# Score products as two 64-row tiles of TensorE's array, and the constant rows of the keys written by DMA

## The reference

```python
x = x + 0.5 * ffn(layernorm(x))
x = x + attn(layernorm(x))
x = x + 0.5 * ffn(layernorm(x))

# ffn: 8 experts, each takes the 128 tokens with the highest gate value
affinity = softmax(x @ gate_w)
gating, index = top_k(affinity_T, 128)
h = silu(x_sel @ Wg) * (x_sel @ Wu)
x_out = zeros.at[b_idx, index].add((h @ Wd) * gating)

# attn: 16 heads of 8 features
inner, outer, v = x @ Wi, x @ Wo, x @ Wv
attn = softmax(inner @ outer.T / scale) * aperture * expression
attn = attn / (attn.sum(-1) + 1e-8)
combined = rotate(attn @ v)              # a rotation of pairs, times factors of each head
return combined @ Wout
```

## Time and profile before

| | us |
|---|---|
| median of 3 runs (517.5 to 518.35) | 518.32 |
| span of the profiled execution | 516.1 |
| TensorE busy | 427.1 |
| VectorE busy | 400.4 |
| ScalarE busy | 239.9 |
| GpSimd busy | 68.6 |

### The profile page before, as it was taken

The page is one execution under the profiler, slowest core; times in us unless marked ns, Lnnn a source line. Parts: engine busy times, 40 slices in busy tenths (PEclk is TensorE's granted clock), DMA queues, the critical chain, the costliest instruction groups (busy, mean ns, idle before and its releaser), DMA issues.

```text
span 516.1 us, 7820 instructions
## 1 busy us (share of the span) xinstructions
PE 427.1 (83%) x2252; PEld 250.8 (49%) x2252; DVE 400.4 (78%) x841; ACT 239.9 (46%) x439; POOL 68.6 (13%) x105
## 2 busy tenths in 40 slices
PE   2605999995588899999999999999996506999995
PEld 2501557773454445555555545554553402567773
DVE  6698848899689987778777777777655598768884
ACT  2400443330341267777676777766784201543332
POOL 5510002149000010000000000000002500001100
PEclk9999999998788799999999999999999655999999
DMA  5000012210058810111111111110110000012212
GB/s 166 1 0 1 1 30 62 61 31 0 4 213 276 297 61 25 37 37 43 42 42 42 42 42 42 42 42 1 35 31 0 0 0 2 1 33 59 61 32 81
DMA packets 24749, 26.03 MB, mean 50 GB/s; under 512 B 3634, under 2 KB 16438, under 8 KB 24726
## 3 DMA queue, kind: packets, MB, share of 16 engines
q1 hardware_dynamic: 24726, 25.74, 16.0%
HBM read 16.16 MB, written 9.44 MB: 50 GB/s over the span
## 4 chain that ended last, share of the span: by engine, by line
PE 69%; DVE 25%; issue 3%; ACT 2%; DMA 1%; DVEq 0%; ACTq 0%
PE ps L1133 12%; PE ps L1158 12%; PE ps L1148 10%; DVE neg_max L807 6%; PE ps L999 5%; PE ps L1035 5%; DVE heads_out L707 3%; PE ps L1018 3%; PE ps L1020 3%; PE ps L1019 3%; DVE values L704 3%; PE ps L1050 2%; PE ps L1051 2%; PE ps L960 2%; DVE probs L746 2%
## 5 line engine op out<-in xcount | busy, mean ns | idle before, releaser
L807 DVE TENSOR_REDUCE neg_max<-ps 128x1 f32<-128x512 f32 x256 | 163.4, 684 | 38.9 <-PE ps L1133 38.9
L597 ACT ACTIVATE probs<-ps 128x512 f32<-128x512 f32 x256 | 137.8, 598 | 64.6 <-PE ps L1148 62.9
L1133 PE MATMUL ps<-k_stack,q_stack 128*128 128x512 f32 x256 | 113.7, 452 | 4.8 <-DVE neg_max L807 3.5
L1148 PE MATMUL ps<-q_stack,k_stack 128*128 128x512 f32 x256 | 100.6, 403 | 0.2 <-ACT probs L597 0.2
L1133 PEld LDWEIGHTS ps<-k_stack,q_stack 128*128 128x128 f32 x256 | 49.0, 192 | 68.8 <-DVE neg_max L807 61.7
L1158 PE MATMUL ps<-probs,v_ext 128*32 128x512 f32 x512 | 68.2, 605 | 0.0
L1148 PEld LDWEIGHTS ps<-q_stack,k_stack 128*128 128x128 f32 x256 | 47.7, 190 | 12.7 <-ACT probs L597 5.7
L523 ACT CAST k_stack<-ps 128x512 fp32r<-128x512 f32 x32 | 17.2, 589 | 67.7 <-PE ps L999 67.7
L451 POOL TENSOR_TENSOR w_lo<-w_gu,w_hi 128x512 fp32r<-128x512 f32 x16 | 20.4, 1279 | 149.7 <-ACT w_hi L510 149.7
L769 DVE TENSOR_TENSOR vae_and_gates<-heads_out,ps 128x512 f32<-128x512 f32 x32 | 21.9, 687 | 19.7 <-ACT heads_out L531 17.7
L746 DVE TENSOR_TENSOR probs<-slot_row,slot 128x1024 f16<-128x1024 f16 x32 | 36.5, 1216 | 0.1
(11 more groups left out here) (151 smaller groups left out, 574.8 us busy)
## 6 DMA issues: line engine op xcount, KB each, us to landing
parts_dram<-part_hi SPq DMA_DIRECT2D x8, 512.0 KB, 3.6
parts_dram<-part_lo SPq DMA_DIRECT2D x8, 512.0 KB, 4.9
q_stack<-parts_dram SPq DMA_DIRECT2D x32, 128.0 KB
k_stack<-parts_dram SPq DMA_DIRECT2D x32, 128.0 KB
w_gu<-in_L_ffn_Wg_dram SPq DMA_DIRECT2D x16, 128.0 KB, 2.1
w_gu<-in_L_ffn_Wu_dram SPq DMA_DIRECT2D x16, 128.0 KB, 2.2
wd_sb<-in_L_ffn_Wd_dram SPq DMA_DIRECT2D x16, 128.0 KB, 2.2
x<-in_L_attn_x_dram SPq DMA_DIRECT2D x4, 256.0 KB, 3.8
```

What stands on the lines that cost most here:

```text
L597: nc.scalar.activation(probs[:, u // HG, u % HG, :], ps[:, RING + ring_bank(step, u), :], ACT.Exp, scale=SCORE_SCALE).then_inc(probs_ready, 1)
L807: nc.vector.tensor_reduce(neg_max[:, g, qt, col:col + 1], ps[:, ring_bank(step, u), :], AX.X, ALU.max, negate=True).then_inc(max_taken, 1)
L1133: nc.tensor.matmul(ps[:, ring_bank(step, u), :], q_stack[:, g, pp, chunk(qt)], k_stack[:, g, 2 * pp + jj, :], start=True, stop=True).then_ ...
L1148: nc.tensor.matmul(ps[:, RING + ring_bank(step, u), :], k_stack[:, g, j, chunk(c)], q_stack[:, g, j // 2, :], start=True, stop=True).then_ ...
```

## The change

The score products use 64 rows instead of 128. `q_stack` and `k_stack` become the two halves of one tensor, in which the even head of a pair has rows 0 to 63 and the odd head rows 64 to 127: 32 rows of parts, 31 rows that are zero in the keys, and row 63 (127) with the ones in the keys and the maxima in the queries. The score products take all 64 rows, the maximum products the first 63, so that the row of the maxima needs no clearing. A product's rows fix the part of the array that it uses. The maxima are taken in another order (`max_unit`), so that a score product and the maximum product behind it lie in different halves. The constant rows are written once by four DMAs on SP's queue, from a row of 64 ones and from a zero row in DRAM; GpSimd's three fills of `k_stack` and the clearing DMAs go. `place` gets memory of its own, and the picked tokens lie in both stacks.

```diff
+    PARTS = 4
+    ROWS = PARTS * DH
+    TILE = P // 2
+    MAX_ROW = TILE - 1
...
+        ones_row = sb("ones_row", [1, 64])
-        q_stack = sb("q_stack", [P, G, PAIRS, S], F32R)
-
-        k_stack = sb("k_stack", [P, G, HG, S], F32R)
+        stacks = sb("stacks", [P, 2, G, PAIRS, S], F32R)
+        q_stack, k_stack = stacks[:, 0], stacks[:, 1]
+        place = sb("place", [P, 2, B, S], F32R)
...
+        def max_unit(u):
+
+            return u // HG, (u + 1) % HG
...
             def load_max_rows(n, g):
 
                 sp.wait_ge(max_rows_ready, n + 1)
                 for jj in range(2):
-                    sp.dma_start(q_stack[64 * jj + 32:64 * jj + 33, g].bitcast(F32),
+                    sp.dma_start(q_stack[TILE * jj + MAX_ROW:TILE * jj + TILE, g].bitcast(F32),
                                  max_rows[2 * jj:2 * jj + 2, g % 2, :].bitcast(F32)).then_inc(max_rows_loaded[g], 16)
 
-            sp.wait_ge(scattered[0], B)
-            sp.wait_ge(zero_rows_stored, 16)
-            sp.wait_ge(attention_consts, 3)
-            for g in range(G):
-                clear_max_rows(g)
+            sp.wait_ge(consts_made, 7)
+            zero_floats = zeros[0:2 * G * PAIRS].bitcast(F32)
+            sp.dma_start(zero_row_dram.rearrange("a (p t) -> (a p) t", t=S // 2), zero_floats).then_inc(zero_row_stored, 16)
+            sp.wait_ge(zero_row_stored, 16)
+            sp.wait_ge(ones_row_made, 1)
+            sp.wait_ge(gate_up_done[0], 2 * MI * E)
+            for jj in range(2):
+                at = TILE * jj + MAX_ROW
+                sp.dma_start(k_stack[at:at + 1].bitcast(F32).rearrange("r g pp (a t) -> r (g pp a) t", t=64),
+                             ones_row[:].unsqueeze(1).broadcast_to([1, G * PAIRS * S // 64, 64])).then_inc(k_rows_filled, 16)
+                sp.dma_start(k_stack[TILE * jj + ROWS:at].bitcast(F32).rearrange("r g pp t -> r (g pp t)"),
+                             zero_row_dram.broadcast_to([MAX_ROW - ROWS, G * PAIRS * S])).then_inc(k_rows_filled, 16)
             store_parts(0)
...
                     sp.wait_ge(scores_ready, n * EXP_UNITS + 1)
-                    clear_max_rows((step + 3) % G)
                     load_stacks(b + 1, (step + 3) % G)
...
                 nc.gpsimd.memset(v_ext[:], 0.0).then_inc(pool_consts, 1)
-                pool.wait_ge(gate_up_done[0], 2 * MI * E)
-                nc.gpsimd.memset(k_stack[:].bitcast(F32), 0.0).then_inc(pool_consts, 1)
-                pool.wait_ge(pool_consts, 5)
+                pool.wait_ge(pool_consts, 4)
                 nc.gpsimd.memset(v_ext[:, :, :, :, DH + 1:DH + 2], 1.0).then_inc(attention_consts, 1)
-
-                for jj in range(2):
-                    pool.wait_ge(attention_consts, 1 + jj)
-                    ones_rows = k_stack[64 * jj + 4 * DH:64 * jj + 4 * DH + 1].rearrange("r g (pp jj) t -> r g jj pp t", jj=2)[:, :, jj]
-                    nc.gpsimd.memset(ones_rows.bitcast(F32), 1.0).then_inc(attention_consts, 1)
...
             def max_scores(n, step, u):
 
-                g, qt = step % G, u % C
-
-                jj, pp = u // C // 2, u // C % 2
+                g = step % G
+                qt, j = max_unit(u)
+                rows, pp = slice(TILE * (j % 2), TILE * (j % 2) + MAX_ROW), j // 2
                 pe.wait_ge(max_taken, ring_wait(n, step, u, 3))
-                nc.tensor.matmul(ps[:, ring_bank(step, u), :], q_stack[:, g, pp, chunk(qt)], k_stack[:, g, 2 * pp + jj, :],
+                nc.tensor.matmul(ps[:, ring_bank(step, u), :], q_stack[rows, g, pp, chunk(qt)], k_stack[rows, g, pp, :],
                                  start=True, stop=True).then_inc(max_scores_ready, 1)
...
                 pe.wait_ge(probs_ready, ring_wait(n, step, u, 1))
-                nc.tensor.matmul(ps[:, RING + ring_bank(step, u), :], k_stack[:, g, j, chunk(c)], q_stack[:, g, j // 2, :],
+                rows, pp = slice(TILE * (j % 2), TILE * (j % 2) + TILE), j // 2
+                nc.tensor.matmul(ps[:, RING + ring_bank(step, u), :], k_stack[rows, g, pp, chunk(c)], q_stack[rows, g, pp, :],
                                  start=True, stop=True).then_inc(scores_ready, 1)
...
             pe.wait_ge(xnT_ready[1], B)
+            pe.wait_ge(k_rows_filled, 64)
             first_maxima(0, range(RING))
```

More of the change, by code:

```diff
@@ L141, in macaron_block @@
         z_weight = sb("z_weight", [P, T, H])
-        q_stack = sb("q_stack", [P, G, PAIRS, S], F32R)
-        k_stack = sb("k_stack", [P, G, HG, S], F32R)
+        stacks = sb("stacks", [P, 2, G, PAIRS, S], F32R)
+        q_stack, k_stack = stacks[:, 0], stacks[:, 1]
+        picked = stacks[:].rearrange("p n g q s -> p n (g q s)").rearrange("p n (e b s) -> p n e b s", e=E, b=B)
+        place = sb("place", [P, 2, B, S], F32R)
         v_ext = sb("v_ext", [P, G, C, HG, VW])
@@ L157, in macaron_block @@
         combinedT = xnT
-        picked_hi, picked_lo = (k_stack[:].rearrange("p (n g) j s -> p n (g j s)", n=2)[:, n].rearrange(
-            "p (e b s) -> p e b s", e=E, b=B) for n in range(2))
+        picked_hi, picked_lo = picked[:, 0], picked[:, 1]
         hidden = vae_and_gates[:, 0:2 * MI * B * K].rearrange("p (u m s) -> p u m s", u=2, m=MI)
@@ L165, in macaron_block @@
         wy_lo = part_hi[:].rearrange("p u q (b d) -> p u (q b) d", d=D)[:, :, B:2 * B]
-        place = q_stack[:].rearrange("p (u b) q s -> p u (b q) s", u=2)
         moeT = combined[:].rearrange("p (b c) d -> p b (c d)", b=B)
@@ L170, in macaron_block @@
         row_i = sb("row_i", [P, 2], I32)
-        parts_dram = nc.dram_tensor("parts_dram", [2, B, H, DH, 4, S], F32, kind="Internal").ap()
-        zero_rows_dram = nc.dram_tensor("zero_rows_dram", [PAIRS, S], F32, kind="Internal").ap()
+        parts_dram = nc.dram_tensor("parts_dram", [2, B, H, DH, PARTS, S], F32, kind="Internal").ap()
+        zero_row_dram = nc.dram_tensor("zero_row_dram", [1, G * PAIRS * S], F32, kind="Internal").ap()
         ps = ctx.enter_context(nc.psum_tensor("ps", [P, 8, 512], F32))
@@ L182, in macaron_block @@
         attention_consts = sem("attention_consts")
+        ones_row_made, zero_row_stored, k_rows_filled = sem("ones_row_made"), sem("zero_row_stored"), sem("k_rows_filled")
         x_loaded = [sem(f"x_loaded{b}") for b in range(B)]
@@ L185, in macaron_block @@
         attn_weights_loaded = sem("attn_weights_loaded")
-        zero_rows_stored = sem("zero_rows_stored")
         out_stored = sem("out_stored")
@@ L249, in macaron_block @@
         EXP_UNITS = C * HG
+        STACK_DMAS = 2 * 2 * 16
         def ring_bank(step, u):
             return (MAX_UNITS * step + u) % RING
+        def max_unit(u):
+            return u // HG, (u + 1) % HG
         def ring_wait(n, step, u, first_step):
@@ L304, in _ @@
             load_experts(0)
-            sp.wait_ge(consts_made, 7)
-            sp.dma_start(zero_rows_dram, zeros[0:PAIRS].bitcast(F32).rearrange("p (a t) -> p a t", a=1).broadcast_to([PAIRS, 2, S // 2])).then_inc(zero_rows_stored, 16)
             def store_parts(b):
@@ L317, in load_stacks @@
             def load_stacks(b, g):
-                for qk in range(2):
+                for qk, stack in enumerate((q_stack, k_stack)):
                     rows = parts_dram[qk].rearrange("b (g pp jj) d a t -> g jj b (d a) pp t", g=G, pp=PAIRS)
                     for jj in range(2):
[L321 to L325, removed]
-                for jj in range(2):
-                    sp.dma_start(q_stack[64 * jj + 4 * DH:64 * jj + 4 * DH + 1, g].bitcast(F32), zero_rows_dram).then_inc(stacks_loaded[g], 16)
+                        sp.dma_start(stack[TILE * jj:TILE * jj + ROWS, g].bitcast(F32),
+                                     rows[g, jj, bass.ds(b, 1)].squeeze(0)).then_inc(stacks_loaded[g], 16)
             def load_max_rows(n, g):
@@ L385, in _ @@
             nc.gpsimd.memset(ones[:], 1.0).then_inc(pool_consts, 1)
+            nc.gpsimd.memset(ones_row[:], 1.0).then_inc(ones_row_made, 1)
             pool.wait_ge(pool_consts, 1)
@@ L463, in _ @@
             attention_constants()
-            pool.wait_ge(attention_consts, 3)
+            pool.wait_ge(attention_consts, 1)
             pool.wait_ge(gates_ready, 2)
@@ L804, in take_max @@
                 g = step % G
-                col, qt = u // C, u % C
+                qt, j = max_unit(u)
                 dve.wait_ge(max_scores_ready, n * MAX_UNITS + (u + 1))
+                col = 2 * (j % 2) + j // 2
                 nc.vector.tensor_reduce(neg_max[:, g, qt, col:col + 1], ps[:, ring_bank(step, u), :], AX.X, ALU.max, negate=True).then_inc(max_taken, 1)
@@ L848, in _ @@
             norm_apply(1, B - 1, steps)
-            dve.wait_ge(attention_consts, 3)
+            dve.wait_ge(attention_consts, 1)
             add_bias(0)
@@ L1175, in attend @@
                 if has_max:
-                    pe.wait_ge(stacks_loaded[(g + 2) % G], (b + (step + 2) // G) * 96 + 96)
```

(3 more changed lines are left out.)

## The result

The changed kernel takes 521.44 us (median of 4 runs, 520.84 to 522.39) beside 518.34 for the kernel before (4 runs, 517.5 to 518.65): a ratio of 1.0062, 95% interval 1.0046 to 1.0078. It is 0.6% slower, where 495.5 us was forecast and a loss had a chance of 0.06. The profiled execution has a span of 519.7 us.

The account below looks back on a forecast made before the run. The prediction took TensorE's chain as the bound, with GpSimd's fill in the first expert layer's tail. Gains 12.2 + 9.5 + 0.7 = 22.4 us: span 516.1 to 493.7, plus 2.2 is 495.9, forecast 495.5; range 487 to 508.

Parts of the forecast that it names:

- The fill by GpSimd: First expert layer's tail, last down product to first addition to `x`: 20.0 us falls to 7.8, gaining 12.2 us.
- The fill by DMA: Constant rows of `k_stack` on SP's queue: zeros done about 125 us, 145 if three times slower; costed at nothing.
- Rival (d): Something late, DMAs or the clock in the norms, replaces the fill: up to 5 of 12 us lost, 500; chance 0.12.
- The steps: Attention steps with 64-row score products: 13.34 us falls to 12.65, 0.68 each, 9.5 us over 14 steps.
- changes of shape: Transposes of 128 rows between 64-row products: four new changes a step, 0 to 0.4 us, taken as 0.2.
- The last maximum: In a plain stretch it waits for VectorE to free the first maximum's bank, starting at 1.30 us instead of 1.51.
- the stretch: Plain stretch between two blocks of value products in a step: 3.06 us falls to 2.96.
- row tiles overlap: Score and maximum products in different array halves run at once, so a pair costs one slot of 0.235 us.
- Rival (b): TensorE's clock falls to 1.2 GHz in attention: about 19 us a step, 584 us if all 14; chance 0.06.
- The last two steps: Final two attention steps, with scores only: gain taken as 0.7 us, bounds 0 to 2.

Follow-up runs that it names:

- the reordered version: Maxima taken in head order 0,1,2,3 instead of 1,2,3,0, built on the change with 32-row zero fills: 492.59 us, ratio 0.9508 to the kernel before.

## Why the prediction was wrong, point by point

- **The fill by GpSimd, 12.2 us:** right. The tail fell from 20.0 to 7.82 us, and to 7.82 also where the fills alone were replaced.
- **The fill by DMA, costed at nothing:** this is the step that failed. I took the price from a 512 KB store that lands in 4.9 us and its bound from three times that, and noted that no row shows 31 rows. The row was no neighbour: a store keeps most engines busy (a share of 0.82 from 134 to 140 us in the version with 32 rows), 31 rows run on one, at 27 GB/s. The bound had to be the rate of one engine: the two fills need 38 us and end at about 154, not 125 or 145, and the first store is issued at 132. I also took the cover up to the first store and not what a store has to wait for: its last share, behind the fill on the engine that is late. That turns the sign. Of the 25.9 us between forecast and measurement the fill is 21.3: with 32 rows the same kernel has 500.2 us. The stretch that grew by 23.9 us holds 1.0 us that the version with 32 rows loses too.
- **Rival (d)** named this place, at 5 of 12 us given back. It named late DMAs but not why they would be late, and its size was four times too small: 21.3 us.
- **The steps, 12.65 us, 9.5 us in all:** right in kind, with the gain put a little low. A plain step has 12.43, which is the sum before the 0.2 for changes of shape; with every fourth, longer step the mean is 12.57. The last maximum, forecast at 1.30, starts at 1.28; the stretch, forecast at 2.96, takes 2.94. The thirteen steps between the marks save 11.4 us, 0.88 each where 0.68 was forecast. The changes of shape are not free, but they show only in the two stretches with transposes (0.53 us from the transposes of the maxima to the next maximum, 210.66 to 211.19 in the 32-row version, against 0.36 before, 206.25 to 206.61), where they lie partly under other waits.
- **That row tiles overlap** had no row in the trace of before. The products that start at the same 0.01 us in the reordered version show it, and the Trainium skill ("TensorE: Matmul & The Clock Gate", Packing small matmuls), which says that matmuls on different row groups run at once, is borne out.
- **Rival (b), the clock:** it did not come in the steps, but before them. In the version with 32 rows, step 0's transposes come 10.5 us earlier than before and step 2's only 7.2: 3.3 us are lost between, and the changed kernel loses the same 3.2. The windows of the 32-row version give the clock as 0.50 from 152 to 164 us, 0.78 from 164 to 170 and 0.58 from 170 to 180; the kernel before has 0.50 from 164 to 170, 0.96 from 170 to 176, 0.72 from 176 to 182 and 1.00 from there on. There the 63-row maxima come one by one at VectorE's rate. I had this stretch in the earlier trace rows and used it only for the steps. That the clock is what costs the 3.3 us is read from these windows; no run changes it alone.
- **The last two steps, 0.7 us:** 0.1 measured from step 15's transposes to the end.
- **That 500.2 lies inside the range of 487 to 508** is partly luck, for errors offset each other. In the spans the version with 32 rows wins 7.2 us up to step 2, where 12.2 were forecast, then 11.3 in the steps, where 9.5 were, and nothing to speak of at the end, where 0.7 was.

## What to carry to other kernels

Before a DMA replaces a fill, ask over how many engines its shape spreads: 31 rows, a prime number, ran on one engine (no other prime was tried), and the stores behind them on the queue had to wait for it. Write one row more, or cut the rows in two. And when two products can run side by side, put the one that another engine holds back next to the last one before the next block: here one changed index, worth 7.6 us by the medians.

## What the runs showed of the hardware

- A DMA of 31 rows, in source and destination, ran at 23 to 28 GB/s (a share of 0.06 to 0.07) in pieces of 16, 2 and 1 KB; 30 + 1, 16 + 15 and 32 rows ran on many engines (shares of 0.76, 1.03 and 0.76 from 116 to 122 us; with 32 rows 512 KB land in 5.5 us).
- Behind 31 rows in 16 KB pieces SP issued two stores in 2.37 us, behind 2 KB pieces in 17.59 us, behind 1 KB pieces in 22.16 us.
- With 33 rows a half fed to the products the granted clock was 0.50 for whole steps (200 to 220 us) and 1.00 for others (280 to 300 us). With 63 and 64 rows it stayed at 1.00 from 200 to 300 us, whether the rest of the rows held zeros in the keys or leftovers.
- GpSimd's fills hold VectorE's `tensor_scalar` even where only one row is filled: beside the two one-row fills of the earlier trace rows four of them take 7.86 us instead of 1.67. A one-row fill takes 3.6 us, as long as 128 rows of the same width (3.52 us).
